# Focus block: weighed values in the turned probabilities' PSUM pair, and a new order of ACT, PE and DVE work in a round

## What is computed

```python
for it in range(3):
    qp, kp, vp = curq @ Wqh.T + bqh, k @ Wkh.T + bkh, v @ Wvh.T + bvh
    ai = softmax(_ln(qp) @ _ln(kp).T * scale) @ vp
    if it == 0: attn_out = ai; curq, k, v = curq + ai, kp, vp
    else:       # keep or drop ai by mean(abs(ai - prev)); else the same step
        ...
```

## Time and profile before

| | us |
|---|---|
| median of 3 runs | 7721.05 |
| range of the runs | 7704.44 to 7728.39 |
| the profiled execution | 7713.37 |
| its span in the trace | 7711.6 |
| rounds of the first phase (t = 0 to 23) in the trace, from 1394.95 to 1822.98 | 428.03 |
| rounds of the second phase (t = 0 to 11), from 1915.52 to 2116.96 | 201.44 |

### The profile page before, as it was taken

One profiled execution on the slowest core, in us unless ns is written; L12 is line 12 of the kernel. 1 busy time (PEld: TensorE's weight loads), 2 busy tenths in 40 slices (PEclk: granted clock), 3 DMA queues, 4 the chain that ended last, 5 costly groups with the idle time before them and its releaser, 6 DMA issues. The chain is left out here.

```text
span 7711.6 us, 190413 instructions
## 1 busy us (share of the span) xinstructions
PE 6731.2 (87%) x75040; PEld 4112.0 (53%) x75040; DVE 5364.4 (70%) x8861; ACT 4156.1 (54%) x6107; POOL 2878.0 (37%) x1663
## 2 busy tenths in 40 slices
PE   7989994877777899988898868989889999989898
PEld 5766683443442333333333335667557666767676
DVE  7867465454536999988999954668667777767544
ACT  4555333454535777767777764546444444446433
POOL 3311163332312888867888810136112221211000
PEclk9999996999978999998999989999999999999999
DMA  0000001000001222212222200000000000000000
GB/s 27 0 18 14 2 0 17 2 3 2 3 8 35 71 72 76 75 54 75 71 71 77 72 9 16 11 7 0 3 29 2 2 2 2 2 13 14 14 0 22
DMA packets 117005, 191.55 MB, mean 25 GB/s; under 512 B 39542, under 2 KB 75420, under 8 KB 116060
## 3 DMA queue, kind: packets, MB, share of 16 engines
q1 hardware_dynamic: 116572, 185.25, 7.6%
HBM read 174.99 MB, written 8.09 MB: 24 GB/s over the span
## 5 line engine op out<-in xcount | busy, mean ns | idle before, releaser
L2461 POOL TENSOR_TENSOR m_dBx<-m_dtx,m_Bs 128x1024 f32<-128x1024 f32 x518 | 1212.0, 2357 | 212.3 <-DVE m_hs L2798 170.0
L2798 DVE TENSOR_TENSOR_SCAN m_hs<-m_ps_dA,m_dBx 128x512 f32<-128x512 f32 x1036 | 1207.0, 1206 | 84.0 <-POOL m_dBx L2461 82.1
L2577 PE MATMUL m_ps_y<-m_yc,ident 128*128 128x512 f32 x2072 | 1068.3, 640 | 0.0
L2670 ACT ACTIVATE m_ps_dA<-m_dt,m_A 128x504 f32<-128x504 f32 x1036 | 687.0, 678 | 485.0 <-DVE m_hs L2798 482.3
L1998 POOL TENSOR_TENSOR a_s<-a_s,a_den 128x1024 f32<-128x1024 f32 x128 | 243.7, 1904 | 1141.7 <-DVE a_den L2044 1141.7
L2809 DVE TENSOR_TENSOR m_yc<-m_hs,m_ps_C 128x1024 f32<-128x1024 f32 x518 | 619.9, 1197 | 5.5 <-PE m_ps_C L2560 4.5
L2577 PEld LDWEIGHTS m_ps_y<-m_yc,ident 128*128 128x128 f32 x2072 | 361.7, 194 | 374.0 <-issue 374.0
L2560 PE MATMUL m_ps_C<-m_parts,m_sel 48*128 48x512 bf16 x520 | 205.3, 395 | 198.7 <-DVE m_yc L2809 198.5
L2560 PEld LDWEIGHTS m_ps_C<-m_parts,m_sel 48*128 48x128 bf16 x520 | 48.3, 93 | 608.2 <-DVE m_yc L2809 442.2
L580 POOL TENSOR_TENSOR c_kbd<-c_kf,c_hmask 128x1024 f32<-128x1024 f32 x66 | 125.1, 1895 | 527.5 <-ACT c_kf L493 514.6
L2042 DVE TENSOR_REDUCE a_den<-a_s 128x16 f32<-128x1024 f32 x128 | 156.1, 1219 | 206.7 <-ACT a_s L1950 206.7
(11 more groups left out here) (745 smaller groups left out, 16442.0 us busy)
## 6 DMA issues: line engine op xcount, KB each, us to landing
m_Bs<-m_BC_rows SPq DMA_DIRECT2D x260, 512.0 KB, 3.6
c_kvb<-in_ctxT SPq DMA_DIRECT2D x68, 128.0 KB, 2.1
c_kvb<-in_ctxT SPq DMA_DIRECT2D x17, 256.0 KB, 2.7
out_dram<-X SPq DMA_DIRECT2D x1, 4096.0 KB
m_BC_rows<-m_low SPq DMA_DIRECT2D x34, 64.0 KB, 2.8
m_part_rows<-m_split SPq DMA_DIRECT2D x34, 48.0 KB, 1.7
m_parts<-m_part_rows SPq DMA_DIRECT2D x34, 48.0 KB, 1.7
m_piece<-m_BC_rows SPq DMA_DIRECT2D x34, 32.0 KB, 1.7
```

Of the source, the lines that this page charges most:

```text
L2461: return nc.gpsimd.tensor_tensor(to, one, other, ALU.mult)
L2577: last = nc.tensor.matmul(ps_y[:, m, :], C.ident[:], of[:, m, :], start=s == 0, stop=s == NS - 1)
L2670: nc.scalar.activation(seqs(ps_dA[:, h % 3, :]), seqs(dt[:, par, m, :]), ACT.Exp, scale=A[:, m, s:s + 1]).then_inc(decay, 1)
L2798: nc.vector.tensor_tensor_scan(hs[:, s % HS, m, :], ps_dA[:, (2 * s + m) % 3, :], dBx[:, s % BX, m, :], 0.0, ALU.mult, ALU.add).then_inc(s ...
```

## The change

The weighed values and the denominators are written to `ps_t` in place of `ps_a`. On PE, `turn_probs(t-1, 1)` now waits for `den_read` of the job before, `spread_values(t)` waits for `got_ready` of job t-1, and `project(t+2)` waits only for `var_read`; the wait for `var_read` stands after `masks(t+1)` and no longer ahead of `weigh(t-1)`. On ACT, the logarithm of the variances stands between the second and the third copy of the turned probabilities, and its exponential after the fourth. On DVE, `qs` is an own function, `scale_queries(t+1)`, and stands ahead of `result(t-1)`; `distance(t-2)` stands after the spread keys.

```diff
@@ spread_values
                 pe.wait_ge(kv_taken, j + 1)
-                pe.wait_ge(pT_ready, 4 * j)
+                pe.wait_ge(got_ready, j)
@@ turn_probs
                     pe.wait_ge(v_taken, 2 * j + 2)
+                elif r == 1 and j:
+                    pe.wait_ge(den_read, j)
@@ weigh
-                            nc.tensor.matmul(ps_a[rr, 0, q], vbd[...], pT[:, r, q], start=True, stop=True,
+                            nc.tensor.matmul(ps_t[rr, 0, q], vbd[...], pT[:, r, q], start=True, stop=True,
...
-                    last = nc.tensor.matmul(ps_a[rr, 1, :], vmask[:, 0:32], pT[:, r, :], start=True, stop=True)
+                    last = nc.tensor.matmul(ps_t[rr, 1, :], vmask[:, 0:32], pT[:, r, :], start=True, stop=True)
@@ PE, run
-                    if t + 1 < N:
-                        pe.wait_ge(var_read, j + 2)
                     if t:
                         weigh(ph, t - 1)
                     if t + 1 < N:
                         masks(ph, t + 1)
-                    if t:
-                        pe.wait_ge(den_read, j)
-                        pe.wait_ge(got_ready, j)
+                        pe.wait_ge(var_read, j + 2)
                     if t + 2 < N:
                         project(ph, t + 2)
...
+                pe.wait_ge(den_read, first + N)
+                pe.wait_ge(got_ready, first + N)
                 pe.wait_ge(sums_in, 2 if first else 1)
@@ ACT, spreads
                 nc.scalar.activation(spread[:], ps_a[:], ACT.Ln, bias=eps[:, 0:1]).then_inc(var_read, 1)
+
+            def inverse_spreads():
                 act.drain()
                 nc.scalar.activation(spread[:], spread[:], ACT.Exp, scale=-0.5).then_inc(spread_ready, 1)
@@ ACT, denominators
-                nc.scalar.activation(rden[:], ps_a[:, 1, :], ACT.Ln).then_inc(den_read, 1)
+                nc.scalar.activation(rden[:], ps_t[:, 1, :], ACT.Ln).then_inc(den_read, 1)
@@ ACT, run
                     if t:
-                        take_probs(ph, t - 1)
+                        take_probs(ph, t - 1, (0, 1))
                     if t + 1 < N:
                         spreads(ph, t + 1)
+                    if t:
+                        take_probs(ph, t - 1, (2, 3))
+                    if t + 1 < N:
+                        inverse_spreads()
                     if t < N:
                         exponents(ph, t)
@@ DVE
-            def spread_heads(ph, n):
+            def scale_queries(ph, n):
                 j, _, _ = job(ph, n)
                 dve.wait_ge(normed, j + 1)
                 ts(qs[:], qk[:, j % 3, 0, :], g_q[:, 0:1], be_q[:, 0:1], ALU.mult, ALU.add)
+
+            def spread_heads(ph, n):
...
-                tt(got[it % 2][:, ch, :], ps_a[:, 0, :], rden[:], ALU.mult).then_inc(got_ready, 1)
+                tt(got[it % 2][:, ch, :], ps_t[:, 0, :], rden[:], ALU.mult).then_inc(got_ready, 1)
@@ DVE, run
                         shift(ph, t)
+                    if t + 1 < N:
+                        scale_queries(ph, t + 1)
                     if t:
                         result(ph, t - 1)
+                    if t + 1 < N:
+                        spread_heads(ph, t + 1)
                     if t > 1:
                         distance(ph, t - 2)
-                    if t + 1 < N:
-                        spread_heads(ph, t + 1)
```

More of the change, by code:

```diff
@@ L3204, in weigh @@
                             rr = slice(32 * r, 32 * r + 32)
-                            nc.tensor.matmul(ps_a[rr, 0, q], vbd[:, 4 * t + g, r, :, :].rearrange("p h d -> p (h d)"), pT[:, r, q], start=True, stop=True,
+                            nc.tensor.matmul(ps_t[rr, 0, q], vbd[:, 4 * t + g, r, :, :].rearrange("p h d -> p (h d)"), pT[:, r, q], start=True, stop=True,
                                              skip_group_check=True)
@@ L3385, in exponents, with take_probs @@
                 nc.scalar.activation(s1[:, j % 2, :, :], s1[:, j % 2, :, :], ACT.Exp).then_inc(exped, 1)
-            def take_probs(ph, n):
+            def take_probs(ph, n, turns):
                 j, _, _ = job(ph, n)
@@ L3390, in take_probs @@
                     act.wait_ge(out_done, j)
-                for r in range(RG):
+                for r in turns:
                     act.wait_ge(pT_done, 4 * j + r + 1)
@@ L3622, in spread_heads @@
                 ts(qs[:], qk[:, j % 3, 0, :], g_q[:, 0:1], be_q[:, 0:1], ALU.mult, ALU.add)
+            def spread_heads(ph, n):
+                j, _, _ = job(ph, n)
                 for h in range(HR):
@@ L3665, in run @@
                 N = jobs(ph)
+                scale_queries(ph, 0)
                 spread_heads(ph, 0)
```

## The result

The changed kernel takes a median of 7621.4 us (7617.91 to 7625.12), the kernel before, run beside it, 7712.74 us (7699.78 to 7728.39). The ratio is 0.9885 [0.9873, 0.9898], so 79 to 98 us are gone, 89 in the middle. The forecast was 7654 us with a range of 7628 to 7690: right in direction, too small in size.

A forecast was written before the change was run, and what follows sets the result against it. Each round was taken as a loop of waits, no engine full. Savings of 36.2, 25.6 and 21.3 us by iteration plus 1.8 made 85, less 18 for stalls: 67 off 7721, so 7654 us, range 7628 to 7690.

The forecast's parts named there:

- the term for PE's stalls: PE's unexplained stalls, 0.58 us a round, stay on the new path; 18 us come off the 85 us gain.
- the forecast's clean rounds: Rounds without disturbance: 15.9 us in iteration 0, 16.95 in iteration 1, 15.30 in iteration 2.
- The projection came as told: PE's projection starts behind the masks at about 10.05 us, not 12.17, and takes 1.9 us at full clock.
- Its cause was told too simply: The wait ahead of PE's projection was held for the cause of the 0.50 clock on that stretch.
- The two orders were priced: ACT's earlier logarithm saves 0.43 us a round at the weighing; moving DVE's `qs` saves about 0.45 us.
- `kbd` sets the next scores as told: DVE's `kbd`, delayed by POOL's instructions, holds the next scores until 15.9 us in iteration 0, 16.95 in iteration 1.
- (B): Half clock stays on PE's projection; rounds of 16.7 or 16.95 us, gain 49 us, 7672 us; chance 0.22.
- (C): DVE's `kbd` runs first, POOL's `squares` waits; every round 15.30 us, gain 94 us, 7627 us; chance 0.08.
- (D): PE's own stalls grow to one of 1.7 us in every round; gain 34 us, 7687 us; chance 0.12.
- (E): Slower through PE's instruction supply; at stalls of 5 us a round, 7767 us; chance 0.03.
- (F): No effect, within 0.3%: the loop closes over something unseen, such as the value copies; chance 0.03.

The follow-up runs named there:

- wait behind: Changed kernel with PE's wait for `var_read` moved back to the weighing, behind the wait for `pT_ready`: 7665.8 us, rounds 594.0 us.
- wait ahead: Changed kernel with PE's wait for `var_read` moved back to the weighing, ahead of the wait for `pT_ready`: 7692.4 us, rounds 618.4 us.
- the wait put back: Changed kernel with the projection again waiting for the result (`got_ready`): 7658.3 us, rounds 577.7 us.
- DVE's old order: Changed kernel with DVE's order as before (result, distance, queries, keys): 7663.5 us beside 7719.6, rounds 579.8 us.
- the orders alone: Kernel before with only ACT's and DVE's new orders, PSUM pair and PE's order as before: 7723.2 us beside 7720.6, rounds 636.3 us.

## Why the prediction was right or wrong

**The step that failed** is the term for PE's stalls: "Nothing in the change takes them away, and where they fall in scores or weighing they lie on the new path as on the old. So 30 rounds x 0.6 = 18 us come off." The change does take away the largest share: it leaves the weighing without a wait that stands alone, and its stalls (10.1 us over 6 rounds of the first phase, 14.7 over 9 in the second trace) go, along with stretches at the lower clock behind them. Put back by one wait that no data needs, they cost 35 us (wait behind) or 59 us (wait ahead) of rounds, so their price was too low as well.

**That the sum came near is luck.** The two errors nearly cancel. From its own base, 629.5 us, the forecast has the changed kernel's rounds at 562.5 us; 558.3, 560.8 and 559.2 came, 3 us less in the mean. The 30 rounds lie 13.2, 18.7 and 14.6 us above the forecast's clean rounds, for its 18 us, but what fills this is not what the forecast had: stalls at `spread_values` and in the scores, and the lower clock in iteration 1. Had the weighing's stalls stayed, as it says, 594 us of rounds would have been left (the wait behind), a gain of 40 us.

**What the step does not explain.** Of the 22 us between 67 and 89, 3 are the changed kernel's rounds. Another 5 are the base: the trace that the forecast started from had 629.5 us of rounds, the mean of two is 634.4. About 11 us lie behind the block, where nothing was changed, a term that the forecast put at nothing. Variants of the changed kernel have 5559 to 5580 us there, the kernel before 5569 and 5575, so it moves by more than that between kernels. No experiment settles it, and it stays open, as do the last 3 us.

**The removed wait and the clock.** The projection came as told, at 9.99 us, as the masks end, and in 1.98 us. Its cause was told too simply: the wait put back brings the lower level in eight of 22 rounds. In the kernel before, 64.8 of 428 us ran at that level; after, 6.8 of 372 (22.2 and 19.5 us in its two further traces). No single cause carries it: the wait ahead of the projection, the stalls in the weighing and the pauses ahead of the scores each have it behind them in some run, and their shares in the kernel before were not taken apart.

**ACT's and DVE's part.** The weighing at 6.83 us, `kbd` from 11.56, the copies at 12.01 and `squares` at 13.55 are the forecast to 0.1 us, the result at 10.96 came 0.1 us earlier. The two orders were priced at 0.43 and 0.45 us a round and measured 0.43 and 0.45 in clean rounds.

**What is late next.** `kbd` sets the next scores as told: 16.06 us for the forecast's 15.9 in iteration 0, 17.0 to 17.12 for 16.95 in iteration 1. In iteration 2 the clean round took 14.50 us, not 15.30: from t = 14 on `carry` has one product fewer, which the forecast had overlooked. With the 0.6 us the forecast gave groups of 16.5, 17.5 and 15.9 us; 16.39, 17.02 and 15.20 came, and 16.2 to 16.3, 17.5 to 17.6 and 16.0 to 16.1 in its two further traces.

**The rivals.** (B) did not come at the projection: pauses of 1.30 us stayed ahead of the weighing in all 22 rounds and new ones of 0.75 to 2.6 us came ahead of the scores, but the windows of the first phase are at 1.00. Its mechanism is there all the same where the pauses are longer. Over the 18 traces, the lower level begins in the pause ahead of the scores for `kbd`, or within 2.5 us behind it, in none of the 37 cases with a pause of 1.4 to 2.0 us, in 30 of the 45 with 2.0 to 3.0 us, and in all 11 with more than 3.0 us, which are those of DVE's old order. Of the changed kernel's 26.0 us in the second phase, 15 lie in the three rounds whose scores had waited 2.56 us, though in the first phase three such pauses brought none. So the two new orders are worth more than their length. The Trainium skill ("TensorE: Matmul & The Clock Gate", section "HAM oscillation — how this bites in real kernels") has the clock go down in a loop whose waits between bursts are longer than those of the changed kernel. It does not say that each pause brings this, as the prediction read it for its 7672 us; the runs agree with the page as far as longer pauses go, but the 1.68 us ahead of the projection brought the lower level too, in eight of 22 rounds. (C) did not come: DVE waited, and the run that made POOL wait shows what C would have given, 533.6 us of rounds. The Trainium skill ("SBUF — State Buffer", section "Who interferes with whom") has the engine that starts first hold the port for its whole instruction; the trace agrees: in the round shown, the `kbd` instruction that starts at 1485.34 under the POOL instruction of 1485.15 ends 0.3 us after it. (D), growing stalls, had the right place to look and the wrong sign here; the orders alone behave like it: 2.4 to 2.9 us in 11 rounds, and the lower clock behind them, eat their whole gain. (E) and (F) did not come.

## What to carry to other kernels

A wait for an instruction's data costs its length; a wait ahead of a long run of small TensorE instructions can also cost their supply. Put such waits where the engine idles anyway, let the one that ends last be the one in the weight load, and count the "issue" rows of before by the wait ahead of them before calling them constant. And when an order is tried by itself, as the two orders here, it can show nothing although it is worth 46 us beside the other edit.

## What the runs showed of the hardware that was not expected

- PE's instructions come in packets of 16,384 bytes, one for 256 of them (76 packets for 19,426 instructions). A stall for want of them ends 1.2 to 1.6 us after the packet has landed. In the 256 instructions of the weighing it costs 2.0 to 3.0 us when a wait that stands alone ends 0.1 us before them, 1.1 to 2.1 us when it ends 1.0 us before, nothing when there is no such wait. That the queue ahead of PE fills during a wait in a weight load, and not during one that stands alone, is my reading of this; the queue itself is not in the trace.
- A pause of 1.68 us ahead of the projection left the clock at its full level in 14 of 22 rounds. A stall of 2.4 us or more behind a pause of 1.4 us was followed by the lower level, and rounds of 20 to 23 us, each time (21 rounds of two kernels). All 11 pauses of more than 3.0 us ahead of the scores had it, none of the 37 of 1.4 to 2.0 us.
- Why a stall falls into just these rounds and not their neighbours is not settled, beyond that its place goes with the stream of instructions.
